# Record encoder on one core: token loads ahead of two pair loads, two rounds of digits and one compare moved

## The reference

```python
def step(carry, xt):
    h, c = carry
    g = xt @ Wx + h @ Wh + b
    i, f, gg, o = jnp.split(g, 4, axis=-1)
    c = jax.nn.sigmoid(f) * c + jax.nn.sigmoid(i) * jnp.tanh(gg)
    h = jax.nn.sigmoid(o) * jnp.tanh(c)
    return ((h, c), None)
...
m_from = lstm_last(base_emb[from_seq], seq_Wx, seq_Wh, seq_b)
m_to = lstm_last(base_emb[to_seq], seq_Wx, seq_Wh, seq_b)
...
x = jnp.concatenate([ne[nums], fe[fr]], axis=-1)   # per feature, then its LSTM
...
return jax.nn.relu(feats @ reduce_W + reduce_b)
```

## Time and profile before

| | us |
|---|---|
| median of 3 runs | 1714.61 |
| lowest and highest run | 1713.93, 1714.71 |
| the profiled execution, its own time | 1714.94 |
| its span in the trace | 1713.1 |
| PE busy | 1610.2 (94%) |
| DVE busy | 1509.0 (88%) |
| ACT busy | 1314.0 (77%) |
| POOL busy | 955.3 (56%) |

### The profile page before, as it was taken

The page is one execution under the profiler, slowest core; times in us unless marked ns, Lnnn a source line. Parts: engine busy times, 40 slices in busy tenths (PEclk is TensorE's granted clock), DMA queues, the critical chain, the costliest instruction groups (busy, mean ns, idle before and its releaser), DMA issues.

```text
span 1713.1 us, 57020 instructions
## 1 busy us (share of the span) xinstructions
PE 1610.2 (94%) x23780; PEld 619.1 (36%) x23780; DVE 1509.0 (88%) x1573; ACT 1314.0 (77%) x2011; POOL 955.3 (56%) x473
## 2 busy tenths in 40 slices
PE   3799999999999999999999999999999999999997
PEld 0233333333333333333333333333333333333334
DVE  6788988989988989988989988988988988988984
ACT  4577777877777877777877778877778877778874
POOL 1445666776666776666754444554444554444553
PEclk8899999999999999999999999999999999999999
DMA  8678789898889898889788789899889888788870
GB/s 285 223 253 261 248 263 276 264 276 271 256 268 284 250 284 260 270 264 284 251 287 262 260 263 277 260 275 267 273 265 280 256 277 274 256 267 273 248 241 24
DMA packets 165793, 444.19 MB, mean 259 GB/s; under 512 B 45728, under 2 KB 103584, under 8 KB 132640
## 3 DMA queue, kind: packets, MB, share of 16 engines
q1 hardware_dynamic: 162112, 439.63, 81.8%
q0 software_dynamic: 2560, 0.15, 0.6%
q10 hardware_dynamic: 864, 0.75, 0.1%
HBM read 423.42 MB, written 6.82 MB: 251 GB/s over the span
## 4 chain that ended last, share of the span: by engine, by line
PE 53%; DVE 17%; ACT 15%; issue 9%; POOL 2%; DVEq 0%; POOLq 0%; ACTq 0%
PE e_ps L479 16%; PE ab L619 11%; PE f_ps L619 9%; PE ab L511 7%; DVE kept L493 7%; ACT gate L673 5%; DVE f_ps L705 5%; DVE seq_c L710 4%; ACT f_ps L671 3%; PE ab L425 3%; ACT tanh_c L664 3%; PE ab L560 2%; POOL ig L697 2%; ACT f_ps L673 2%; PE ab L570 2%
## 5 line engine op out<-in xcount | busy, mean ns | idle before, releaser
L697 POOL TENSOR_TENSOR ig<-gate 128x1024 f32<-128x1024 f32 x192 | 411.9, 2145 | 696.3 <-ACT seq_x L432 293.7
L479 PE MATMUL e_ps<-hot,tab 128*32 128x512 bf16 x8448 | 527.5, 384 | 61.6 <-DVE kept L493 56.8
L493 DVE SCALAR_TENSOR_TENSOR kept<-high,cst,e_ps 128x1024 f32<-128x1024 uint8 x352 | 449.1, 1276 | 49.6 <-PE e_ps L479 43.8
L619 PE MATMUL ab<-seq_h,seq_wh 64*64 64x512 f32 x3024 | 401.2, 590 | 0.0
L479 PEld LDWEIGHTS e_ps<-hot,tab 128*32 128x32 bf16 x8448 | 214.0, 97 | 486.8 <-issue 342.7
L469 DVE TENSOR_SCALAR hot<-low,cst 128x4096 bf16<-128x4096 bf16 x256 | 320.6, 1281 | 13.2 <-PE e_ps L479 13.2
L731 POOL TENSOR_TENSOR seq_h<-gate,tanh_c 128x1024 f32<-128x1024 f32 x128 | 308.9, 2414 | 31.8 <-ACT tanh_c L664 31.6
L673 ACT ACTIVATE gate<-ab,nwf_bias 128x512 f32<-128x512 f32 (+2 forms) x384 | 188.4, 553 | 166.2 <-PE ab L570 103.0
L671 ACT ACTIVATE gate<-ab 128x1024 f32<-128x1024 f32 x256 | 262.5, 1026 | 17.6 <-PE ab L619 8.8
L664 ACT ACTIVATE tanh_c<-seq_c 64x512 f32<-64x512 f32 (+1 forms) x384 | 241.9, 630 | 29.8 <-POOL nwf_h L731 22.1
L664 ACT ACTIVATE gate<-ab 64x512 f32<-64x512 f32 (+1 forms) x384 | 228.5, 595 | 9.4
(11 more groups left out here) (99 smaller groups left out, 1809.1 us busy)
## 6 DMA issues: line engine op xcount, KB each, us to landing
low<-low_digits SPq DMA_DIRECT2D x256, 1024.0 KB
low<-low_bytes SPq DMA_DIRECT2D x96, 512.0 KB
tok<-seq_tokens SPq DMA_DIRECT2D x128, 384.0 KB
high<-high_digits SPq DMA_DIRECT2D x1408, 32.0 KB
nwf_hq<-nwf_h SPq DMA_DIRECT2D x62, 128.0 KB
raw<-in_indices SPq DMA_DIRECT2D x32, 176.0 KB
low_digits<-low_of SPq DMA_DIRECT2D x32, 88.0 KB, 3.2
nwf_hq<-nwf_h SPq DMA_DIRECT2D x62, 32.0 KB, 3.0
```

What stands on the lines that cost most here:

```text
L479: last = nc.tensor.matmul(e_ps[32 * g:32 * g + 32, i, :], tab[:, part, 2 * m + ty, :], hot[:, p % HOT_RING, g, i, :], start=(part == 0), s ...
L493: nc.vector.scalar_tensor_tensor(out=kept[:, p % KEPT_RING, :, :], in0=wanted, scalar=cst[:, C_HIGH:C_HIGH + 1], in1=e_ps[:, :, :], op0=AL ...
L619: last = nc.tensor.matmul(flat(bank)[to:to + 64, cols], lhs(rows, half, block), rhs(rows, block, a, b), start=start, stop=stop)
L697: nc.gpsimd.tensor_tensor(ig[:, cols], gates[0][:, n % 2, cols], gates[1][:, n % 2, cols], ALU.mult).then_inc(ig_ready, 1)
```

## The change

On SP the loads of the tokens for seq cells 2 and 3 move ahead of the loads of pairs 2 and 3. On DVE the digits of round 1 move from cell 0 to cell 1, and the digits of round 2 from cell 3 to cell 4. Pair 3 is compared at the head of cell 1, behind `add_c(0)`, and no longer in cell 0. POOL's first `ig` waits for the compare of pair 2 instead of pair 3. Stores of digits and loads of indices on SP follow their rounds. No operation is added or removed.

```diff
-ROUND_AT = {(0, 3)[_r - 1] if _r < 3 else NUMBER["nwf", _r - 2, 0]: _r for _r in range(FIRST_ROUNDS, NWF_T)}
+ROUND_AT = {1 if _r == 1 else NUMBER["nwf", _r - 2, 0]: _r for _r in range(FIRST_ROUNDS, NWF_T)}
...
+LATE_PAIR = 3
...
-                for p in range(1, LOW_RING):
+                for p in range(1, HOT_RING):
+                    load_pair(sp, p)
+
+                for s in range(2, 2 + AHEAD):
+                    load_tokens(sp, s)
+                for p in range(HOT_RING, LOW_RING):
                     load_pair(sp, p)
                 sp.dma_start(few_in[:, :, :], few).then_inc(s_few, 16)
                 load_raw(sp, 2)
-                for s in range(2, 2 + AHEAD):
-                    load_tokens(sp, s)
...
+                    if n == 1:
+                        compare_pair(dve, LATE_PAIR)
                     pairs = PAIRS_AT[n]
-                    compared = [p + HOT_RING for p in pairs if p + HOT_RING < ALL_PAIRS]
+                    compared = [p + HOT_RING for p in pairs if p + HOT_RING < ALL_PAIRS and p + HOT_RING != LATE_PAIR]
...
-                    for p in PAIRS_AT[n][:2][-1:]:
+                    for p in (PAIRS_AT[n][:1] if n == 0 else PAIRS_AT[n][:2][-1:]):
                         pool.wait_ge(hot_ready, min(p + HOT_RING + 1, ALL_PAIRS))
```

## The result

The changed kernel takes 1709.02 us (median of 14 runs, 1707.11 to 1711.76), beside 1712.62 us (14 runs, 1710.33 to 1714.71) for the kernel before on the same chip: a ratio of 0.9978 with an interval of 0.9972 to 0.9985. That is 3.6 us or 0.22% faster, just above what this measurement tells from no change. The forecast was 1707.0 in a range of 1702.5 to 1712, so the time is in the range and the direction is right. But the forecast rested on a gain of 7.6 us, and 3.6 us is half of it. It is off by only 2.0 us because a second error pulls the other way: the three runs that it started from had a median of 1714.61, and the 14 runs beside the changed kernel, which take in these three, have 1712.62. A gain that was 4.0 us too large and a base that was 2.0 us too high leave 2.0. That the number came so near is in part luck.

What follows compares the result with a forecast made beforehand. TensorE bounds from 149 us; in the first 100 us it waits longest for DVE's `kept`. Terms -4.1 - 4.1 - 1.4 + 2.0 = -7.6 us from 1714.94 give 1707.3, as a median 1707.0; range 1702.5 to 1712.

Steps and rivals of the forecast that it cites:

- Cells 0 and 1, -4.1: Start: earlier tokens end DVE's 4.99 us idle time, 7.3 us won in cell 0, part given back in cell 1.
- the better end of -6.3: Cells 0 and 1: the bound of that term if POOL and DVE miss each other.
- Cell 3, -4.1: Cell 3: seven digits instructions leave, compares run without a break and POOL's `new_h` waits; 4.1 us won.
- Clock, -1.4: TensorE's half-clock stretch after cell 3's wait: half of 2.9 us won, with 0 and -2.9 as ends.
- Cell 4, +2.0: Cell 4: digits between the compares of pairs 11 and 12 cost 2.0 us, from 0 to +3.5.
- Cell 5, 0: Cell 5: no term in the sum; a longer TensorE wait there was named only in (c).
- (c): Slower: cell 4 becomes the new stall, cell 5's wait grows to about 6.9, clock falls; +3.6 us, chance 0.06.
- The base: Starting time: the profiled execution's 1714.94 us, with the median of the runs 0.33 lower.
- Its own signs: Checks in cells 0 to 5: idle time gone, `add_c` ends, pair 8's wait under 3.5, cell 4's POOL wait above 2.5.
- (a): Clock stays up and POOL misses DVE in cell 1: -11.3 us, 1703.3, chance 0.16.
- (b): Cells 0 and 1: transfers limit pairs 2 to 5, start given back, only digits remain; -3.1 us, 1711.5, chance 0.15.
- (d): No change: TensorE's own work sets the early pace, waits change owner; within 1 us of 1714.6, chance 0.03.

Runs made afterwards that it cites:

- e2_loads_only: The kernel before with only the token loads moved ahead of pairs 2 and 3: 1709.25 us, 0.9985 of before.
- e3_all_slots: Changed kernel; round 1's digits before the first cell, round 2's in cell 7, cell 1's `seq_hot` before `kept`, POOL's `new_h` behind cell 3's compares: 1707.14 us, 0.9981 of before.
- e2_pool_cell3: Changed kernel with one added wait: in cell 3 POOL starts `new_h` only after both compares: 1706.21 us, 0.9963 of before.
- e3_pool_cells34: Changed kernel with POOL's `new_h` waiting for the compares in cell 3 and in cell 4: 1704.89 us, 0.9967 of before.
- e4_slot_and_pool: Changed kernel with round 2's digits behind `kept` of pair 7 in cell 3, and POOL's `new_h` behind pair 9's compare: 1706.85 us, 0.9964 of before.

## Why the prediction was right, and where its size was not

**Cells 0 and 1, -4.1: right by its path, and near in size.** 47.0 us in the changed kernel against 51.2 and 50.8 in the two traces of before: -4.2 and -3.8. Over all traces with the same start it is nearer -3.3 (47.7 against 51.0). The order of landing in the full queue gave pair 2's digits at 28.0, and the compare began at 28.67. The block of `seq_hot` from 35.9 was found at 36.19. The Trainium skill, "SBUF — State Buffer", section "Who interferes with whom", has it that whoever issues first holds the pair and the other fully blocks; this row agrees, 2.64 us against 0.74. What the forecast did not see is that the loads alone bring as much (`e2_loads_only`: 47.3), and that without the collision DVE would have stood before pair 5: in `e3_all_slots`, where neither `seq_hot` nor the digits meet POOL in cell 1, it waits 3.01 us for that pair's low digits. So the better end of -6.3 was not to be had from these loads as they landed there.

**Cell 3, -4.1: the term that failed.** The step was: "Without them the compares of pairs 8 and 9 follow `seq_hot` without a break, so DVE keeps the port and POOL's `new_h` waits". POOL did not wait for the second compare. The look-up of pair 8 waited 4.85 us and not 2.7; the cell got 2.3 to 3.1 us shorter, clock included, against 5.5. Of the 4.1 us of digits, 2.1 were a collision, and the collision stayed; only the 1.98 of work left. The row on which that step leaned, POOL's 5.11 us at 53.21, shows POOL waiting behind three DVE instructions in a row. It was real, but it was one of two outcomes, and the forecast took it for a rule. Where the order is forced, the forecast's numbers are there: waits of 2.98, 2.77 and 2.76 and cells of 12.7, 13.9 and 13.7 us (`e2_pool_cell3`, `e3_pool_cells34`, `e3_all_slots`).

**Clock, -1.4: not there.** In the changed kernel the look-up of pair 8 still takes 2.73 us, and 2.34 in the second trace. With POOL held back it came once in four: 1.48 in `e2_pool_cell3`, yet 2.48 in `e3_pool_cells34` and 2.75 in `e3_all_slots` and `e4_slot_and_pool`, behind waits of 2.98, 2.77, 2.76 and 2.75. For a wait of that size either outcome has to be carried in the range, as it was.

**Cell 4, +2.0: near in size (+1.5), and half right by its path.** The forecast left open which of the two would wait. It was DVE's compare, 3.37 us for 1.28; POOL's product, which waits for that compare, started 1.16 us late and still came last before `add_c`, but by 0.22 us and not by more than 2.5. With the compare first (`e3_pool_cells34`) `add_c` waits 2.52 us for POOL, and the cell takes 13.8 us. So either order costs about the same here. What differs is TensorE's wait behind it, 4.16 or 2.07 us.

**Cell 5, 0: missed.** The forecast named this wait only in rival (c), at 6.9 us. It is 4.16 us, and TensorE works at half clock behind it; against the second trace of before the cell is 1.3 to 2.0 us longer (9.4 and 10.1 against 8.1), and the first trace hid that by a clock stretch of its own. With the terms from the first trace of the changed kernel against the second of before: -3.8 for cells 0 and 1, -0.3 for cell 2, -2.3, +1.5, +1.3, which is -3.6. That this is the 3.6 us of the medians is partly chance, since one trace of a kernel stands up to 2.4 us from the next at cell 9.

**The base.** 1714.94 and 1714.61 were both high for this kernel. A forecast of the difference, set on a median of three, takes over its error: about 2 us here, as much as a term. This time the error hid half of the gain that was missing.

**Its own signs.** The 4.99 us are gone, and both `add_c` ends are where they were expected. The look-up of pair 8 waits longer than 3.5 us, and cell 4's `add_c` waits less than 2.5 for POOL: these two missed, and they are the two that test cells 3 and 4. DVE also waits 1.23 us for low digits in cell 0, which was named as a sign of being wrong; but the forecast's own sum had it wait there from 27.35 to 28.0, so that sign contradicted the sum. The wait in cell 5 stays under 5 us.

**The rivals.** (a), -11.3, needed POOL and DVE to miss each other in cell 1; by `e3_all_slots` that time would have gone into the wait for pair 5. (b) is nearest in size, -3.1, and was wrong in its place: the start was not given back, the digits were. (c) held in part: the wait in cell 5 and its clock are real, at a quarter of its price. (d) falls, 0.9978.

## What to carry to other kernels

In a full transfer queue the order of the loads is a schedule of its own: add up bytes up to each first use, and put ahead what the next blocked engine wants; here that alone gave most or all of the gain (0.9985, against 0.9978 for the whole change), with no operation changed. Moving work of an engine that shares a port with another moves the collision along with it, so find out which instruction will be hit next, and if the other engine's work is not wanted soon, make it wait on purpose: an added wait of 2.5 us on POOL made cell 3 shorter by 2.1 to 3.4 us, though that the whole kernel gained by it is not shown. And before a forecast of 0.3% is set on one trace, look at what in it is chance; a second trace of the same kernel differed by 2.4 us at cell 9 and by 5.0 us in its span.
